# Selective-scan block: where the factor B of a state step is applied (rows of delta u on ScalarE and GpSimd, or a diagonal inside TensorE's product)

## The chip, the cores and the metric

One NeuronCore of a Trainium2 chip runs the whole program. The metric is the device time of one execution in microseconds (us). The kernel before took 759.8 us, the median of 3 runs (757.31 to 759.98).

## What is computed

The input is x with 4 sequences of 1024 tokens and 128 channels. First comes a layer norm with scale and shift, then a Mamba-like block (`_selective_scan`) with 256 channels and 16 states, a gate and an output product, and after it a second layer norm and a mixture of 8 experts of which each token takes 2. The part that matters here, cut from the reference:

```python
xp = u @ x_proj_w
delta = softplus(xp[..., :64] @ dt_proj_w + dt_proj_b)
Bm = xp[..., 64:80]
Cm = xp[..., 80:]
dA = exp(delta[..., None] * A)
dBu = delta[..., None] * Bm[:, :, None, :] * u[..., None]
h = dA_t * h + dBu_t          # per token, for each channel d and state n
y = einsum('bdn,bn->bd', h, C_t)
```

For one state n, dBu is delta u, (token x channel), with each token's row multiplied by that token's B of state n. Everything is fp32.

## The kernel before

**Segments and steps.** The 4096 tokens are cut into 8 segments (SEGS) of 512 tokens; a sequence is 2 segments, so the odd segments (1, 3, 5, 7) go on from the state that the even one before them left. A segment has 16 steps, one for each state n, so there are 128 steps k. A step has 2 halves a of 128 channels each. A half of a step is called a gap; a segment has 32 gaps.

**A step, engine by engine.** delta u of a segment lies in `duT` with tokens on the partitions: 4 chunks (CS) of 128 tokens by 256 channels. B lies beside it in `BT`, one column per chunk and state.

- `scale_in(k)` multiplies the rows of duT by the step's column of BT and writes them to `S`. In segments 0 to 6 a ScalarE instruction scales one chunk of 256 channels (L976), and one GpSimd instruction scales the last chunks (L522): `pool_chunks(k)` gives GpSimd 1 and 2 chunks in turn in segments 0 and 1, and 1 in segments 2 to 6. ScalarE has the rest.
- `turn_in(k, a)` on TensorE turns the four scaled blocks of 128 tokens by 128 channels into channels by tokens with `turn`, a matmul in transpose mode (L571), into one of 3 PSUM banks (DBU_BANKS).
- `decay(k, a)` on ScalarE computes dA for one half (L987).
- `scan(k, a)` on VectorE runs the recurrence over the 512 tokens (L1335): dA from SBUF, dBu from the PSUM bank, the result into `ring`.
- GpSimd multiplies both halves by the step's row of C (L542), which a DMA has spread over the partitions.
- `add_state(k, a)` on TensorE adds them up in PSUM with four more `turn` matmuls (L571), three steps later (LAG).

**The last segment is another case already.** In segment 7 `pool_chunks` is 0. ScalarE multiplies the identity matrix by the step's column of BT (L979), four 128x128 diagonals a step, and `turn_in` uses `product`, an ordinary fp32 matmul (L567), with the block of duT as the stationary operand and the diagonal as the moving one. That product scales and turns in one operation.

**Order.** Every engine runs a list written out by hand. Per gap TensorE issues `turn_in(k + 1, a)`, an `add_state`, and `gap_work`. ScalarE issues `scale_in(k + 2)` at the head of a step, then per half `decay(k + 2, a)` and `gap_work`. VectorE issues `scan(k, a)` and `gap_work`. GpSimd issues `scale_in(k + 2)`, the product with C, and its scatters. `gap_work` spreads the rest of the block over the gaps: `front` prepares the segment after (layer norm, two convolutions as 8 tap products of 512 columns, the gates), `project` computes its delta, B, C and duT (softplus needs an exponential and a logarithm, so ScalarE loads two function tables a segment, at gap 18), `tail` and `routing` work on the segment before (output product, second norm, router, choice of experts).

**What holds them together.** `turn_in(k, a)` waits for all of the step's scaling and for the scan that last used its bank, three halves back. `decay` waits for a scan six halves back (DA_SLOTS). `scale_in(k)` waits for step k - 3 to have been turned (S_SLOTS). At the first step of a segment `scale_in` waits on ScalarE and on GpSimd for `read["dT1"]`, which VectorE gives with the second half of duT (L1078, in gap 27). VectorE overwrites a duT slot only when the scaling of the segment two back is done. The expert part, from about 540 us on, uses the same engines one tile after another; it shares the memory of S.

Of the kernel before, what the change touches and what calls it, by code (L numbers as in the profile page):

```python
# [7 lines left out]
ALU = mybir.AluOpType  # L8
ACT = mybir.ActivationFunctionType
# [3 lines left out]
P = 128  # L13
BATCH, SEQ, HID = 4, 1024, 128
MLP, NSTATE, DTRANK, CONVK = 256, 16, 64, 4
EXPERTS, INTER, TOPK = 8, 352, 2
NTOK = BATCH * SEQ
HALVES = MLP // P
# [6 lines left out]
LN_EPS = 1e-5  # L25
PROJ = DTRANK + 2 * NSTATE
GAPS = 2 * NSTATE
RING, S_SLOTS, DBU_BANKS, DA_SLOTS, C_GROUP, LAG = 6, 3, 3, 6, 4, 3

INNER = [(c * P, min(P, INTER - c * P)) for c in range(-(-INTER // P))]  # L30
NIN = len(INNER)
# [16 lines left out]
def wait(eng, signal, count):  # L48
    if not (isinstance(count, int) and count <= 0):
        eng.wait_ge(signal, count)  # L50


def pool_chunks(k):

    s = k // NSTATE
    return 1 + k % 2 if s < 2 else int(s < SEGS - 1)


def act_scaled(k):

    return sum(CS - pool_chunks(j) for j in range(k + 1))


def pool_scaled(k):
    return sum(pool_chunks(j) > 0 for j in range(k + 1))


def adaln_kernel(nc, xT_d, w1_d, w2_d, wo_d, xproj_d, dtw_d, alog_d, conv_d, cols_d, bo_d, router_d,
# [5 lines left out]
    with ctx:  # L74
        def sb(name, shape, dt=fp32):
            return ctx.enter_context(nc.sbuf_tensor(name, shape, dt))

        def sem(name):
            return ctx.enter_context(nc.semaphore(name))
# [63 lines left out]
        soft = sb("soft", [P, 3, HALVES, BANK])  # L143
        rv, ev, lw = (soft[:, k] for k in range(3))
        delta = sb("delta", [P, 2, HALVES, BANK])
        S = sb("S", [P, S_SLOTS, CS, MLP])
        dA = sb("dA", [P, DA_SLOTS, BANK])
        Cb = sb("Cb", [P, 2, C_GROUP, BANK])
        ring = sb("ring", [P, RING, HALVES, BANK])
# [56 lines left out]
        def db(k, a):  # L206
            return bank(2 + (k * HALVES + a) % DBU_BANKS)
# [17 lines left out]
        def PO(k):  # L225
# [20 lines left out]
        av_ready, e_ready, lw_ready, w_ready, softplus_step, delta_ready = (  # L246
            sem(n) for n in ("av_ready", "e_ready", "lw_ready", "w_ready", "softplus_step", "delta_ready"))
        c_stored, c_loaded = sem("c_stored"), [sem(f"c_loaded{k}") for k in range(2)]
        scaled_act, scaled_pool, turned_in, da_ready, scanned, kept, prod_ready, summed, y_out, x1_ready = (
            sem(n) for n in ("scaled_act", "scaled_pool", "turned_in", "da_ready", "scanned", "kept", "prod_ready", "summed",  # L250
                             "y_out", "x1_ready"))
        route, prob_exp, chosen_ready, places_ready, place = (
            sem(n) for n in ("route", "prob_exp", "chosen_ready", "places_ready", "place"))
# [173 lines left out]
        def _(pool):  # L427
# [83 lines left out]
                        scatter_ready(f)  # L511
                    scatter(f, (gap - 9) // 3 // TOPK, (gap - 9) // 3 % TOPK)

            def scale_in(k):
                s, n = divmod(k, NSTATE)
                own = pool_chunks(k)
                if own:
                    if n == 0:
                        pool.wait_ge(read["bt"], s + 1)
                        pool.wait_ge(read["dT1"], s + 1)  # L520
                    wait(pool, turned_in, HALVES * (k - S_SLOTS + 1))
                    nc.gpsimd.tensor_tensor(S[:, k % S_SLOTS, CS - own:, :], duT[:, s % 2, CS - own:, :],  # L522
                                            BT[:, s % 2, CS - own:, n:n + 1].to_broadcast([P, own, MLP]), ALU.mult
                                            ).then_inc(scaled_pool, 1)

            pool.wait_ge(mod_step, MOD_STEPS)
            for window in (-2, -1):
                for gap in range(GAPS):
                    gap_work(gap, window)
            scale_in(0)  # L530
            scale_in(1)
            for k in range(STEPS):
                s, n = divmod(k, NSTATE)
                if k + 2 < STEPS:
                    scale_in(k + 2)
                pool.wait_ge(scanned, (k + 1) * HALVES)
                if s % SEG == 0:
                    nc.gpsimd.tensor_copy(state[:, n, :], ring[:, k % RING, :, BANK - 1]).then_inc(kept, 1)
                    pool.wait_ge(kept, s // SEG * NSTATE + n + 1)
                group_, own = divmod(k, C_GROUP)  # L540
                pool.wait_ge(c_loaded[group_ % 2], 16 * (group_ // 2 + 1))
                nc.gpsimd.tensor_tensor(ring[:, k % RING], ring[:, k % RING],  # L542
                                        Cb[:, group_ % 2, own, :].unsqueeze(1).to_broadcast([P, HALVES, BANK]),
                                        ALU.mult).then_inc(prod_ready, 1)
                gap_work(2 * n, s)
                gap_work(2 * n + 1, s)
# [18 lines left out]
        def _(pe):  # L565
# [3 lines left out]
            def turn(out, block_in, start=True, first=0):  # L569
                at = slice(first, first + block_in.shape[0])  # L570
                return nc.tensor.matmul(out, block_in, ident[at, at],  # L571
                                        is_transpose=True, start=start, stop=True, skip_group_check=True)
# [128 lines left out]
            def turn_in(k, a):  # L701


                if a == 0:
                    pe.wait_ge(scaled_act, act_scaled(k))
                    pe.wait_ge(scaled_pool, pool_scaled(k))
                wait(pe, scanned, HALVES * k + a - DBU_BANKS + 1)
                s = k // NSTATE
                for c in range(CS):
                    if s < SEGS - 1:  # L710
                        last = turn(db(k, a)[:, c * P:(c + 1) * P], S[:, k % S_SLOTS, c, a * P:(a + 1) * P])
                    else:
                        last = product(db(k, a)[:, c * P:(c + 1) * P], duT[:, s % 2, c, a * P:(a + 1) * P],
                                       S[:, k % S_SLOTS, c, 0:P])
                last.then_inc(turned_in, 1)

            def add_state(k, a):
# [141 lines left out]
        def _(act):  # L859
# [39 lines left out]
            def project(gap, f):  # L899
                if gap == 12:  # L900
                    act.wait_ge(filled["bt"], f + 1)
                    wait(act, scaled_pool, pool_scaled((f - 1) * NSTATE - 1))
                    nc.scalar.copy(BT[:, f % 2].rearrange("p c n -> p (c n)"), FB[:, 0:CS * NSTATE]).then_inc(read["bt"], 1)
                if gap in (5, 8):
                    a = (gap - 5) // 3
                    act.wait_ge(filled[f"dt{a}"], f + 1)
                    wait(act, delta_ready, f * HALVES)
                    nc.scalar.activation(ev[:, a, :], FB, ACT.Abs, bias=cols[:, 3, a:a + 1]).then_inc(av_ready, 1)  # L908
                    nc.scalar.activation(rv[:, a, :], FB, ACT.Relu, bias=cols[:, 3, a:a + 1]).then_inc(read[f"dt{a}"], 1)  # L909
                if gap in (9, 10):  # L910
                    a = gap - 9
                    act.wait_ge(av_ready, f * HALVES + a + 1)
                    nc.scalar.activation(ev[:, a, :], ev[:, a, :], ACT.Exp, scale=-1.0).then_inc(e_ready, 1)
                if gap == 18:
                    act.wait_ge(e_ready, (f + 1) * HALVES)
                    nc.scalar.activation(lw[:, :, :], ev[:, :, :], ACT.Ln, bias=1.0).then_inc(lw_ready, 1)  # L916
                if gap in (12, 21):
                    a = int(gap == 21)
                    act.wait_ge(read["bt"], f + 1)
                    wait(act, delta_ready, f * HALVES + a)  # L920
                    nc.scalar.activation(FB, ev[:, a, :], ACT.Identity, bias=1.0).then_inc(w_ready, 1)
# [46 lines left out]
            def scale_in(k):  # L968
                s, n = divmod(k, NSTATE)
                if n == 0:  # L970
                    act.wait_ge(read["bt"], s + 1)
                    act.wait_ge(read["dT1"], s + 1)
                wait(act, turned_in, HALVES * (k - S_SLOTS + 1))
                for c in range(CS - pool_chunks(k)):
                    if s < SEGS - 1:
                        nc.scalar.activation(S[:, k % S_SLOTS, c, :], duT[:, s % 2, c, :], ACT.Identity,  # L976
                                             scale=BT[:, s % 2, c, n:n + 1]).then_inc(scaled_act, 1)
                    else:
                        nc.scalar.activation(S[:, k % S_SLOTS, c, 0:P], ident[:, :], ACT.Identity,  # L979
                                             scale=BT[:, s % 2, c, n:n + 1]).then_inc(scaled_act, 1)  # L980

            def decay(k, a):
                s, n = divmod(k, NSTATE)
# [68 lines left out]
        def _(dve):  # L1052
# [15 lines left out]
            def project(gap, f):  # L1068
                if gap in (19, 20, 22, 23):
                    softplus((gap - 19) // 3, (gap - 19) % 3, f)  # L1070
                if gap in (25, 27):
                    a = (gap - 25) // 2
                    dve.wait_ge(filled[f"dT{a}"], f + 1)
                    dve.wait_ge(read[f"uT{a}"], f + 1)
                    if f > 1:
                        dve.wait_ge(scaled_act, act_scaled((f - 1) * NSTATE - 1))
                        dve.wait_ge(scaled_pool, pool_scaled((f - 1) * NSTATE - 1))
                    V.tensor_tensor(duT[:, f % 2, :, a * P:(a + 1) * P], uT[:, :, a * P:(a + 1) * P],  # L1078
                                    FB.rearrange("p (c d) -> p c d", c=CS), ALU.mult).then_inc(read[f"dT{a}"], 1)

# [431 lines left out]
```

## Time and profile before

| | |
|---|---|
| median of 3 runs | 759.8 us |
| profiled execution, its own time | 758.83 us |
| its span, first to last instruction | 756.2 us |
| granted TensorE clock, mean | 0.966 |
| busy share: TensorE, its weight loads, VectorE, ScalarE, GpSimd | 85%, 71%, 73%, 71%, 72% |
| first scan, last step of the chain that feeds the experts | 64.0 us, about 540 us |

The busy shares are averages over the set-up, the 128 steps and the experts. The five numbers lie close together, so they don't say which engine sets the pace of a stage; that is read from the start times of instructions that follow each other and from the waits. A TensorE matmul's duration in the trace holds its latency, so a row of "x4" lasts longer than it keeps the next one waiting: the distance between two starts is what one costs.

### The profile page before, as it was taken

The page shows a single profiled execution, that of the slowest core. Times are in us where ns is not written, and L with a number is a line of the kernel's source. Part 1 is how long each engine was busy: PE and PEld are TensorE (multiplying, and loading weights), DVE is VectorE, ACT ScalarE, POOL GpSimd, SP SyncE. Part 2 cuts the span into 40 slices and gives each one's busy share as a digit, 9 for nine tenths or more (in the row PEclk, how much of TensorE's full clock was granted, in tenths as well). Part 3 has the DMA queues.
Part 4 walks back from the last instruction along what each step waited for, and adds up shares of the span by engine and source line. Part 5 has one row for each costly group of instructions (what it writes and reads, how often), then busy time and mean ns, then how long its engine had stood idle before and what let it go on. Part 6 is the DMA issues. An engine that isn't in the chain of part 4 may idle for free.

```text
span 756.2 us, 14740 instructions
## 1 busy us (share of the span) xinstructions
PE 639.5 (85%) x4563; PEld 537.0 (71%) x4563; DVE 551.7 (73%) x1170; ACT 538.6 (71%) x1024; POOL 542.3 (72%) x519
## 2 busy tenths in 40 slices
PE   3768899989888989988988985899688997899994
PEld 3334766867857767766776774889577886899983
DVE  5066779899888998987989988999544574365552
ACT  3167989979987997996997997868226644465640
POOL 3055979989899899999999999978615454544431
PEclk9999999999999999999999999999789999999997
DMA  6020345355534633643344433586011122222544
GB/s 218 2 112 2 95 111 151 100 155 185 165 97 122 166 96 97 170 118 101 91 122 125 128 94 96 150 224 160 23 34 55 56 61 59 65 67 63 151 151 146
DMA packets 72492, 82.93 MB, mean 110 GB/s; under 512 B 7088, under 2 KB 63472, under 8 KB 68320
## 3 DMA queue, kind: packets, MB, share of 16 engines
q1 hardware_dynamic: 66944, 70.78, 34.6%
q0 software_dynamic: 4320, 9.12, 3.5%
q10 hardware_dynamic: 1152, 2.10, 0.7%
q8 instruction: 38, 0.62, 0.3%
q14 instruction: 38, 0.31, 0.1%
HBM read 52.19 MB, written 29.78 MB: 108 GB/s over the span
## 4 chain that ended last, share of the span: by engine, by line
PE 41%; ACT 32%; DVE 10%; issue 9%; POOL 3%; another core or an unknown queue 2%; DMA 2%; SPq 0%; ACTq 0%; DVEq 0%; POOLq 0%
PE psum L567 24%; PE psum L571 16%; ACT S L976 11%; ACT dA L987 10%; DVE ring L1335 4%; POOL ring L542 1%; ACT xn L881 1%; ACT L916 1%; ACT soft L908 1%; ACT soft L916 1%; ACT soft L909 1%; ACT L987 1%; ACT u L886 1%; ACT hT L863 1%
## 5 line engine op out<-in xcount | busy, mean ns | idle before, releaser
L542 POOL TENSOR_TENSOR ring<-ring,Cb 128x1024 f32<-128x1024 f32 x128 | 302.9, 2368 | 15.7 <-DVE ring L1335 10.4
L987 ACT ACTIVATE dA<-delta,A 128x512 f32<-128x512 f32 x256 | 178.6, 716 | 12.1 <-DVE ring L1335 12.0
L571 PEld LDWEIGHTS psum<-ident,S 128*128 128x128 f32 x896 | 107.4, 145 | 109.9 <-issue 75.8
L571 PE MATMUL psum<-ident,S 128*128 128x128 f32 x896 | 142.1, 284 | 45.8 <-issue 24.6
L571 PE MATMUL psum<-ident,ring 128*128 128x128 f32 x1088 | 164.5, 283 | 12.4 <-DMA ring<-results 6.7
L1335 DVE TENSOR_TENSOR_SCAN ring<-dA,state,psum 128x512 f32<-128x512 f32 x128 | 158.0, 1266 | 1.4 <-PE psum L571 1.0
L1335 DVE TENSOR_TENSOR_SCAN ring<-dA,psum 128x512 f32<-128x512 f32 x128 | 150.6, 1207 | 10.8 <-PE psum L571 6.8
L976 ACT ACTIVATE S<-duT,BT 128x256 f32<-128x256 f32 x320 | 139.3, 502 | 26.5 <-DVE duT L1078 17.8
L559 POOL DMA_INDIRECT results<-xn,result_at x71 | 68.7, 968 | 108.7 <-DVE xn L1462 68.1
L571 PEld LDWEIGHTS psum<-ident,ring 128*128 128x128 f32 x1088 | 132.7, 147 | 14.2 <-DMA ring<-results 7.4
L567 PE MATMUL psum<-uT,S 128*128 128x128 f32 x852 | 109.7, 280 | 0.5 <-issue 0.5
L567 PEld LDWEIGHTS psum<-uT,S 128*128 128x128 f32 x852 | 103.0, 196 | 1.5 <-issue 1.5
L1031 ACT COPY S<-gateup_w 128x736 f32 x71 | 57.0, 804 | 45.5 <-PE psum L567 37.8
L522 POOL TENSOR_TENSOR S<-duT,BT 128x256 f32<-128x256 f32 x112 | 75.7, 677 | 8.7 <-DVE duT L1078 7.7
L1467 DVE TENSOR_TENSOR S<-S,psum 128x384 f32<-128x384 f32 x71 | 39.3, 553 | 56.6 <-ACT S L1041 35.1
L454 POOL DMA_INDIRECT token_rows<-h2r,pos x64 | 65.0, 1016 | 17.6 <-issue 9.0
L1041 ACT ACTIVATE S<-psum 128x384 f32<-128x384 f32 x71 | 34.8, 490 | 56.2 <-PE psum L567 42.0
L567 PE MATMUL psum<-hT,w1c 128*128 128x512 f32 x128 | 67.7, 626 | 6.3 <-ACT u L886 3.5
L567 PE MATMUL psum<-soft,S 128*128 (+1 forms) x426 | 60.0, 277 | 9.9 <-DVE S L1467 6.3
L567 PEld LDWEIGHTS psum<-soft,S 128*128 128x128 f32 (+1 forms) x426 | 53.2, 192 | 11.4 <-issue 11.3
L1444 DVE COPY uT<-psum 128x128 f32<-128x128 f32 x71 | 20.5, 288 | 29.0 <-PE psum L571 18.7
L490 POOL TENSOR_SCALAR xT<-xT,gabo 128x1024 f32<-128x1024 f32 x4 | 11.4, 2871 | 35.5 <-PE psum L571 26.9
(229 smaller groups left out, 835.6 us busy)
## 6 DMA issues: line engine op xcount, KB each, us to landing
Cb<-c_rows SPq DMA_DIRECT2D x32, 1024.0 KB, 6.0
token_rows<-zeros SPq DMA_DIRECT2D x64, 272.0 KB, 7.0
uT<-token_rows SPq DMA_DIRECT2D x71, 68.0 KB
ring<-results SPq DMA_DIRECT2D x16, 256.0 KB, 3.4
xT<-in_xT SPq DMA_DIRECT2D x4, 512.0 KB, 5.2
out_T<-xT ACTq DMA_DIRECT2D x8, 256.0 KB
stage<-in_xT SPq DMA_DIRECT2D x6, 256.0 KB, 8.3
gateup_w<-in_gate SPq DMA_DIRECT2D x1, 1408.0 KB, 9.3
```

Of the source, the lines that this page charges most:

```text
L454: nc.gpsimd.indirect_dma_start(token_rows, bass.IndirectOffsetOnAxis(ap=pos[:, j, g * CS + c:g * CS + c + 1], axis=0), h2r[:, j, g * CS + ...
L522: nc.gpsimd.tensor_tensor(S[:, k % S_SLOTS, CS - own:, :], duT[:, s % 2, CS - own:, :], BT[:, s % 2, CS - own:, n:n + 1].to_broadcast([P, ...
L542: nc.gpsimd.tensor_tensor(ring[:, k % RING], ring[:, k % RING], Cb[:, group_ % 2, own, :].unsqueeze(1).to_broadcast([P, HALVES, BANK]), AL ...
L559: nc.gpsimd.indirect_dma_start(results, bass.IndirectOffsetOnAxis(ap=result_at[:, t % (2 * XS_SLOTS):t % (2 * XS_SLOTS) + 1], axis=0), ob[ ...
L567: return nc.tensor.matmul(out, lhsT, rhs, start=start, stop=stop)
L571: return nc.tensor.matmul(out, block_in, ident[at, at], is_transpose=True, start=start, stop=True, skip_group_check=True)
L976: nc.scalar.activation(S[:, k % S_SLOTS, c, :], duT[:, s % 2, c, :], ACT.Identity, scale=BT[:, s % 2, c, n:n + 1]).then_inc(scaled_act, 1)
L987: nc.scalar.activation(dA[:, (k * HALVES + a) % DA_SLOTS, :], delta[:, s % 2, a, :], ACT.Exp, scale=A[:, a, n:n + 1]).then_inc(da_ready, 1)
L1031: nc.scalar.copy(both_w[:, par % 2, :], gateup_w[:, ds(e * 2 * INTER, INTER + NIN * P)]).then_inc(weights_copied, 1)
L1041: nc.scalar.activation(silu[:, par % 2, :], PG(par)[:, 0:NIN * P], ACT.Silu).then_inc(silu_ready, 1)
L1335: V.tensor_tensor_scan(ring[:, k % RING, a, :], dA[:, (k * HALVES + a) % DA_SLOTS, :], db(k, a), state[:, n, a:a + 1] if s % SEG else 0.0, ...
L1467: V.tensor_tensor(innerT[:, par % 2, :], silu[:, par % 2, :], PU(par)[:, 0:NIN * P], ALU.mult).then_inc(inner_ready, 1)
```

## The change

In all segments ScalarE writes the four diagonals of a step, 128x128 each, and TensorE's `product` of duT with them scales and turns. S has 6 slots of half the width in place of 3, so its size is unchanged. GpSimd's `scale_in` is gone with its counts. TensorE waits for `read["dT0"]` and `read["dT1"]` itself at the first step of a segment, ScalarE no longer does; VectorE's wait before it overwrites duT is for TensorE's products.

```diff
-RING, S_SLOTS, DBU_BANKS, DA_SLOTS, C_GROUP, LAG = 6, 3, 3, 6, 4, 3
+RING, S_SLOTS, DBU_BANKS, DA_SLOTS, C_GROUP, LAG = 6, 6, 3, 6, 4, 3
...
-        S = sb("S", [P, S_SLOTS, CS, MLP])
+        S = sb("S", [P, S_SLOTS, CS, P])
...
-            def scale_in(k):
...
-                    nc.gpsimd.tensor_tensor(S[:, k % S_SLOTS, CS - own:, :], duT[:, s % 2, CS - own:, :],
-                                            BT[:, s % 2, CS - own:, n:n + 1].to_broadcast([P, own, MLP]), ALU.mult
-                                            ).then_inc(scaled_pool, 1)
...
             def turn_in(k, a):
+                s, n = divmod(k, NSTATE)
+                if n == 0:
+                    pe.wait_ge(read[f"dT{a}"], s + 1)
                 if a == 0:
-                    pe.wait_ge(scaled_act, act_scaled(k))
-                    pe.wait_ge(scaled_pool, pool_scaled(k))
+                    pe.wait_ge(scaled_act, CS * (k + 1))
                 wait(pe, scanned, HALVES * k + a - DBU_BANKS + 1)
-                s = k // NSTATE
                 for c in range(CS):
-                    if s < SEGS - 1:
-                        last = turn(db(k, a)[:, c * P:(c + 1) * P], S[:, k % S_SLOTS, c, a * P:(a + 1) * P])
-                    else:
-                        last = product(db(k, a)[:, c * P:(c + 1) * P], duT[:, s % 2, c, a * P:(a + 1) * P],
-                                       S[:, k % S_SLOTS, c, 0:P])
+                    last = product(db(k, a)[:, c * P:(c + 1) * P], duT[:, s % 2, c, a * P:(a + 1) * P],
+                                   S[:, k % S_SLOTS, c, :])
...
                 if n == 0:
                     act.wait_ge(read["bt"], s + 1)
-                    act.wait_ge(read["dT1"], s + 1)
                 wait(act, turned_in, HALVES * (k - S_SLOTS + 1))
-                for c in range(CS - pool_chunks(k)):
-                    if s < SEGS - 1:
-                        nc.scalar.activation(S[:, k % S_SLOTS, c, :], duT[:, s % 2, c, :], ACT.Identity,
-                                             scale=BT[:, s % 2, c, n:n + 1]).then_inc(scaled_act, 1)
-                    else:
-                        nc.scalar.activation(S[:, k % S_SLOTS, c, 0:P], ident[:, :], ACT.Identity,
-                                             scale=BT[:, s % 2, c, n:n + 1]).then_inc(scaled_act, 1)
+                for c in range(CS):
+                    nc.scalar.activation(S[:, k % S_SLOTS, c, :], ident[:, :], ACT.Identity,
+                                         scale=BT[:, s % 2, c, n:n + 1]).then_inc(scaled_act, 1)
...
                     if f > 1:
-                        dve.wait_ge(scaled_act, act_scaled((f - 1) * NSTATE - 1))
-                        dve.wait_ge(scaled_pool, pool_scaled((f - 1) * NSTATE - 1))
+                        dve.wait_ge(turned_in, HALVES * (f - 1) * NSTATE)
```

## Rows read from the trace of the kernel before

**Rows 1.** The page's parts 1 and 4: busy time, and the chain by engine.
```profile
PE 639.5 (85%) x4563; PEld 537.0 (71%) x4563; DVE 551.7 (73%) x1170; ACT 538.6 (71%) x1024; POOL 542.3 (72%) x519
PE 41%; ACT 32%; DVE 10%; issue 9%; POOL 3%; another core or an unknown queue 2%; DMA 2%; SPq 0%; ACTq 0%; DVEq 0%; POOLq 0%
```

**Rows 2.** Windows: the stretch, its length, busy us (and instructions) by engine, granted clock.
```profile
61.00:119.00 58.00, 48.93 (x317) 37.50 (x317) 44.46 (x46) 54.30 (x105) 50.02 (x47) 0.97 0.30 85
119.00:180.00 61.00, 56.97 (x397) 44.57 (x395) 55.96 (x71) 55.90 (x111) 57.29 (x44) 1.00 0.42 119
302.00:363.00 61.00, 53.89 (x369) 42.88 (x367) 52.10 (x80) 54.00 (x108) 57.24 (x62) 0.97 0.45 120
424.00:479.00 55.00, 41.41 (x306) 35.07 (x305) 48.44 (x76) 46.48 (x91) 51.41 (x56) 0.97 0.48 125
479.00:540.00 61.00, 56.41 (x478) 53.16 (x475) 56.45 (x109) 44.54 (x101) 53.08 (x36) 1.00 0.55 142
```

**Rows 3.** The scans (L1335), all of them, then timeline rows at two segment starts.
```profile
L1335 DVE TENSOR_TENSOR_SCAN ring<-dA,psum x128: 1185/1209/1223, 64.0 to 480.5; 128x512 f32<-128x512 f32 x128
L1335 DVE TENSOR_TENSOR_SCAN ring<-dA,state,psum x128: 1248/1270/1281, 119.4 to 534.4; 128x512 f32<-128x512 f32 x128
...
421.53 2.32 DVE L1335 TENSOR_TENSOR_SCAN ring<-dA,psum 128x512 f32<-128x512 f32 x2
...
481.63 2.42 DVE L1335 TENSOR_TENSOR_SCAN ring<-dA,state,psum 128x512 f32<-128x512 f32 x2
```

**Rows 4.** Groups by line and shape: busy us, mean ns, idle before and its releasers.
```profile
L571 PE MATMUL psum<-ident,S 128*128 128x128 f32 x896 | 142.1, 284 | 45.8 <-issue 24.6 <-ACT S L976 14.6 <-POOL S L522 3.3
L976 ACT ACTIVATE S<-duT,BT 128x256 f32<-128x256 f32 x320 | 139.3, 502 | 26.5 <-DVE duT L1078 17.8 <-PE psum L571 6.0 <-issue 2.7
L567 PE MATMUL psum<-S,duT 128*128 128x128 f32 x256 | 34.6, 279 | 1.8 <-DVE ring L1335 1.6
L979 ACT ACTIVATE S<-ident,BT 128x128 f32<-128x128 f32 x64 | 20.2, 387 | 2.6 <-DVE duT L1078 2.6
L522 POOL TENSOR_TENSOR S<-duT,BT 128x256 f32<-128x256 f32 x96 | 59.1, 616 | 8.7 <-DVE duT L1078 7.7
L522 POOL TENSOR_TENSOR S<-duT,BT 128x512 f32<-128x512 f32 x16 | 16.7, 1044 | 0.0
```

**Rows 5.** TensorE's timeline in segment 4: start, us, line, operation and its operands.
```profile
342.50 1.00 PE L571 MATMUL psum<-ident,S 128*128 128x128 f32 x4 [2.15 <-ACT S L976]
343.30 1.06 PE L571 MATMUL psum<-ident,ring 128*128 128x128 f32 x4
344.16 1.06 PE L571 MATMUL psum<-ident,S 128*128 128x128 f32 x4
...
350.05 0.60 PE L571 MATMUL psum<-ident,ring 128*128 128x128 f32 x4
350.48 1.02 PE L567 MATMUL psum<-hT,w1c 128*128 128x512 f32 x2
351.35 0.60 PE L571 MATMUL psum<-ident,S 128*128 128x128 f32 x4
```

**Rows 6.** TensorE's timeline in segment 7.
```profile
482.73 1.06 PE L567 MATMUL psum<-S,duT 128*128 128x128 f32 x8
483.62 0.60 PE L571 MATMUL psum<-ident,ring 128*128 128x128 f32 x4
484.06 1.06 PE L567 MATMUL psum<-S,duT 128*128 128x128 f32 x8
```

**Rows 7.** ScalarE's timeline, from segment 4's table load to its tanh; last, segment 7.
```profile
328.94 1.29 ACT L976 ACTIVATE S<-duT,BT 128x256 f32<-128x256 f32 x3
330.14 0.71 ACT L987 ACTIVATE dA<-delta,A 128x512 f32<-128x512 f32 x1
330.86 1.28 ACT L916 ACT_TABLE_LOAD   x1
...
340.20 0.66 ACT L886 ACTIVATE u<-psum,zhalf 128x512 f32<-128x512 f32 x1
...
496.28 1.26 ACT L979 ACTIVATE S<-ident,BT 128x128 f32<-128x128 f32 x4
497.45 0.71 ACT L987 ACTIVATE dA<-delta,A 128x512 f32<-128x512 f32 x1
```

More of the change, by code:

```diff
@@ L50, in wait @@
         eng.wait_ge(signal, count)
-def pool_chunks(k):
-    s = k // NSTATE
[L56 to L65, printed above, removed]
 def adaln_kernel(nc, xT_d, w1_d, w2_d, wo_d, xproj_d, dtw_d, alog_d, conv_d, cols_d, bo_d, router_d,
@@ L248, in adaln_kernel @@
         c_stored, c_loaded = sem("c_stored"), [sem(f"c_loaded{k}") for k in range(2)]
-        scaled_act, scaled_pool, turned_in, da_ready, scanned, kept, prod_ready, summed, y_out, x1_ready = (
-            sem(n) for n in ("scaled_act", "scaled_pool", "turned_in", "da_ready", "scanned", "kept", "prod_ready", "summed",
+        scaled_act, turned_in, da_ready, scanned, kept, prod_ready, summed, y_out, x1_ready = (
+            sem(n) for n in ("scaled_act", "turned_in", "da_ready", "scanned", "kept", "prod_ready", "summed",
                              "y_out", "x1_ready"))
@@ L512, in gap_work @@
                     scatter(f, (gap - 9) // 3 // TOPK, (gap - 9) // 3 % TOPK)
-            def scale_in(k):
[L515 to L521, printed above, removed]
-                    nc.gpsimd.tensor_tensor(S[:, k % S_SLOTS, CS - own:, :], duT[:, s % 2, CS - own:, :],
-                                            BT[:, s % 2, CS - own:, n:n + 1].to_broadcast([P, own, MLP]), ALU.mult
-                                            ).then_inc(scaled_pool, 1)
             pool.wait_ge(mod_step, MOD_STEPS)
@@ L529, in _ @@
                     gap_work(gap, window)
-            scale_in(0)
-            scale_in(1)
             for k in range(STEPS):
                 s, n = divmod(k, NSTATE)
-                if k + 2 < STEPS:
-                    scale_in(k + 2)
                 pool.wait_ge(scanned, (k + 1) * HALVES)
@@ L701, in turn_in @@
             def turn_in(k, a):
+                s, n = divmod(k, NSTATE)
+                if n == 0:
+                    pe.wait_ge(read[f"dT{a}"], s + 1)
                 if a == 0:
-                    pe.wait_ge(scaled_act, act_scaled(k))
-                    pe.wait_ge(scaled_pool, pool_scaled(k))
+                    pe.wait_ge(scaled_act, CS * (k + 1))
                 wait(pe, scanned, HALVES * k + a - DBU_BANKS + 1)
-                s = k // NSTATE
                 for c in range(CS):
-                    if s < SEGS - 1:
-                        last = turn(db(k, a)[:, c * P:(c + 1) * P], S[:, k % S_SLOTS, c, a * P:(a + 1) * P])
-                    else:
-                        last = product(db(k, a)[:, c * P:(c + 1) * P], duT[:, s % 2, c, a * P:(a + 1) * P],
-                                       S[:, k % S_SLOTS, c, 0:P])
+                    last = product(db(k, a)[:, c * P:(c + 1) * P], duT[:, s % 2, c, a * P:(a + 1) * P],
+                                   S[:, k % S_SLOTS, c, :])
                 last.then_inc(turned_in, 1)
@@ L901, in project @@
                     act.wait_ge(filled["bt"], f + 1)
-                    wait(act, scaled_pool, pool_scaled((f - 1) * NSTATE - 1))
                     nc.scalar.copy(BT[:, f % 2].rearrange("p c n -> p (c n)"), FB[:, 0:CS * NSTATE]).then_inc(read["bt"], 1)
```

## The prediction

> **What bounds the kernel now.** I read the page's shares and the chain first, then windows of one segment each, then the timelines of TensorE and ScalarE inside a segment. The busy shares of the five lie within 14 points and say little; the chain already says more: TensorE 41%, ScalarE 32%, GpSimd only 3% [rows 1]. So GpSimd's work, which the change takes away, is mostly off the path.
>
> The 128 steps run from the first scan at 64.0 us to the last at 534.4 + 1.27 = 535.7. Segment 0 takes 119.4 - 64.0 = 55.4 us, segments 1 to 5 take 421.5 - 119.4 = 302.1 (60.4 each), segment 6 takes 60.1 and segment 7 54.1 [rows 3]. In segments 1 to 5 ScalarE is busy 54 to 56 of 61 us, GpSimd 57, VectorE 52 to 56 [rows 2]. TensorE's busy figure of 54 to 57 overstates its load, since durations hold latency. Its true load comes from distances between starts: four turns take 350.48 - 350.05 = 0.43 us, 0.11 each, and a pair of 512-column products 351.35 - 350.48 = 0.87, 0.43 each [rows 5]. From the code a middle segment has 372 matmul instructions: 256 turns of turn_in and add_state, 84 other short ones, and 32 wide ones (an ordinary fp32 product is two instructions). The windows confirm the number: 397 and 369 in 61 us [rows 2]. So TensorE's floor is 340 x 0.11 + 32 x 0.43 = 37.4 + 13.8 = 51.2 us of 60.4. The 9 us left are waits, for ScalarE's scaling above all: turn_in's turns stood idle 45.8 us, 14.6 put down to L976, 3.3 to GpSimd's scaling and 24.6 to nothing seen [rows 4]; and stretches at half clock behind such waits, as at 343.30, where four turns take 0.86 us after a wait of 2.15 [rows 5]. ScalarE in turn waited 17.8 us at 5 places for VectorE's duT [rows 4]. The pace now is thus set by ScalarE, with TensorE 15% below its limit.
>
> **The change, part by part.**
>
> 1. *GpSimd's scaling goes*: 96 x 0.616 + 16 x 1.044 = 75.8 us of its time [rows 4]. TensorE waited for it 3.3 us in all. I take nothing for it beyond that, since the next point fills the gap: the cover is TensorE itself, which will be later than GpSimd was.
>
> 2. *ScalarE's scaling changes shape.* Three rows of 256 columns take 330.14 - 328.94 = 1.20 us, 0.40 each. Four diagonals take 497.45 - 496.28 = 1.17 us [rows 7]. In segments 2 to 6 that is the same work (-0.03 x 80 = -2 us). In segments 0 and 1 ScalarE had 2.5 chunks a step, 1.0 us: +0.17 x 32 = +5.4 us, on an engine with, after the change, over 5 us a segment to spare, so nothing on the path.
>
> 3. *ScalarE's wait for duT goes*, 17.8 + 2.6 us [rows 4]. It moves to TensorE, which asks for duT at gap 30, when the scan of gap 29, issued behind duT's gap 27 on VectorE, must be done for the bank anyway. Only a wait already there remains. At the very first segment it saves the three scalings between duT and the first turn, 1.2 us: **-1.2 us**. TensorE queues add_state and gap_work behind this wait; with nothing added to it, they lose nothing.
>
> 4. *TensorE: 8 turns a step become 8 ordinary fp32 products.* This is the main term. Segment 7 shows it: L567 with S and duT has 256 instructions, 16 steps x 8 products x 2 [rows 4], while in segments 0 to 6 the 7 x 16 x 8 = 896 turns are one instruction each. And each one costs the same as a turn: a half-step of 8 + 4 instructions comes every 484.06 - 482.73 = 1.33 us, 0.111 each [rows 6]. So a half gets 4 more instructions, a segment 128 more, 128 x 0.11 = 14.1 us.
>  - Segments 1 to 5: floor 51.2 + 14.1 = 65.3 us, which is above the 60.4 of now and above ScalarE (54), VectorE (52 to 56) and GpSimd (57 less 10). TensorE becomes the bound, and the waits for ScalarE are mostly absorbed, because the slower TensorE lets ScalarE run up to its limit of dA slots ahead.
>  - What can't be absorbed: the block around the two table loads. From 330.86 to 340.86 ScalarE needs 10.0 us for gaps 18 to 22 [rows 7]; TensorE will want 5 x 1.33 + 3 taps x 0.87 = 9.3 us for them and then waits for the tanh of gap 22. VectorE has its softplus in the same gaps. I allow 1.5 us there and 1 us elsewhere, 2.5 a segment. Bounds: 0 (segment 7's first six halves show none) and the 9 us of now.
>  - The half clock stretches cost now (1 - 0.97) x 61 = 1.8 us in a typical segment [rows 2]; they follow waits, and where waits are short (window 119 to 180 and segment 7) the clock is 1.00, so I expect them gone; they are part of the 9.
>  - Sum: 5 x (65.3 + 2.5) = 339.0 against 302.1: **+36.9 us**.
>  - Segment 0 has 317 instructions, 28 of them wide: 289 x 0.11 + 28 x 0.43 = 43.8; + 14.1 + 2.5 = 60.4 against 55.4: **+5.0 us**.
>  - Segment 6 prepares no further segment. Its count is 326, 14 wide: 312 x 0.11 + 14 x 0.43 = 40.3, + 14.1 = 54.4. That is below its 60.1 of now. VectorE, 48.4 of 55 us busy, or 53 of 60, is as close [rows 2]. I take 58.5: **-1.6 us** (bounds 55 and 60).
>  - Segment 7 and the experts stay: **0**.
>
> A rule from elsewhere stands against this. The Trainium skill, "TensorE: Matmul & The Clock Gate", Terms (entry xbus), says that transpose mode is 4x faster for FP32. By it each product would cost four turns and the sum would be 3 x 0.11 x 8 x 112 = 296 us. The trace disagrees: two turns, in a segment of the same kernel [rows 4, 6].
>
> 5. *Six slots of S, VectorE's wait for turned_in*: 0. ScalarE's scale_in is held by its place in the list behind decay, not by S (6.0 us of waits for it in all, [rows 4]); VectorE's new wait asks for products of the segment before the running one, done some 25 gaps earlier. No DMA is moved or added; SP's queue sees the same list, later.
>
> Sum: 36.9 + 5.0 - 1.6 - 1.2 = +39.1 us on the profiled execution's 758.8, so 797.9; that execution lies 1.0 under the median of 759.8, so I say **799 us**. (A change of 0.5%, 4 us, is about what can be told from none.)
>
> **The rivals.**
>
> *B: the waits stay on top.* TensorE's products come in bursts that wait for scans three halves back, and VectorE's own bursts then add to the longer work. For it: the idle time is now spread over ScalarE, VectorE and GpSimd, and most of turn_in's is put down to nothing [rows 4]. Against it: at the head of segment 7 TensorE runs without a hole. Price: 7 segments x 14.1 = +99, 858 us; half of it, 822 to 830, if only half is absorbed. Chance 0.08 beyond 822.
>
> *C: faster.* The place is the head of each segment and the table block, where TensorE now waits for ScalarE and ScalarE for duT. If ScalarE's waits of 17.8 + 2.6 us were the pace and TensorE had room for the products, the scan phase would fall by that: 739 us. The point from which it decides: TensorE's floor with the products under ScalarE's 54 us a segment, that is at most 25 added (2.8 / 0.11) instructions where 128 are counted, or a pace of a product under 0.13 us for the pair. Against it: 1.33 us per half in segment 7. Chance 0.03.
>
> *D: no difference*, 756 to 763 us: TensorE's load fits just into its present idle time, as if the 9 us a segment were all usable and my count of the 84 other instructions too high by 45. The windows' counts speak against it. Chance 0.03.
>
> *E: a product costs four turns* when it isn't in segment 7's calm: 759 + 296 = 1055 us. Nothing shows that. Chance 0.01.
>
> **How the numbers follow.** Forecast A (TensorE-bound, waits of 0 to 6 us a segment): with no waits at all and segment 6 at 57 the sum is 24.4 + 2.5 - 3 - 1.2 = +22.7, 782.5; with 6 us a segment, 6 x 3.5 = 21 more than taken, 820. Chance 0.85, of which about 0.81 lies within 785 to 821. The range is **785 to 821**. Slower 0.94 (A, B, E), same 0.03 (D), faster 0.03 (C).
>
> **What the profile would show.** L976 and L522 with S are gone, L979's line has 512 instructions at 0.387 us, L567 with S and duT has 2048. TensorE is over 92% packed in segments 1 to 5, with halves of 1.33 us plus gap_work; the distance between scans two segments apart grows from 121 to some 136 us; clock 1.00 there; GpSimd about 45 of 68 us busy, and its wait for scans up. TensorE's share of the chain rises over 60%, ScalarE's falls under 15%. Segment 7 still takes 54 us. I am wrong if segments 1 to 5 take under 63 us (the count or pace is off) or over 72 (the waits weren't absorbed), or if waits for scans show ahead of turn_in in most halves.

## The result and the profile after

The changed kernel takes 794.7 us (median of 4 runs, 794.17 to 798.23) against 759.9 for the kernel before: a ratio of 1.0469, 95% interval 1.0431 to 1.0507. The profiled execution took 794.17 us with a span of 792.2.

Parts 1 and 4 of the page of the kernel after, against [rows 1]:

```profile
PE 728.3 (92%) x5459; PEld 639.8 (81%) x5459; DVE 555.7 (70%) x1170; ACT 544.3 (69%) x1152; POOL 473.8 (60%) x407
PE 71%; DVE 9%; ACT 7%; issue 5%; POOL 2%; DMA 2%; another core or an unknown queue 1%; SPq 0%; ACTq 0%; DVEq 0%; POOLq 0%
```

TensorE has 5459 - 4563 = 896 more instructions (7 segments x 128) and 71% of the chain, up from 41%. ScalarE's share fell from 32% to 7%.

The scans and the starts of segments 6 and 7, against [rows 3]:

```profile
L1295 DVE TENSOR_TENSOR_SCAN ring<-dA,psum x128: 1184/1210/1222, 65.2 to 516.6; 128x512 f32<-128x512 f32 x128
L1295 DVE TENSOR_TENSOR_SCAN ring<-dA,state,psum x128: 1245/1271/1281, 124.4 to 570.5; 128x512 f32<-128x512 f32 x128
...
456.39 1.21 DVE L1295 TENSOR_TENSOR_SCAN ring<-dA,psum 128x512 f32<-128x512 f32 x1
...
517.74 1.26 DVE L1295 TENSOR_TENSOR_SCAN ring<-dA,state,psum 128x512 f32<-128x512 f32 x1
```

Read as before, they give each stage:

| stage | before | after | difference | forecast |
|---|---|---|---|---|
| start to first scan | 64.0 | 65.2 | +1.2 | -1.2 |
| segment 0 | 55.4 | 59.2 | +3.8 | +5.0 |
| segments 1 to 5 | 302.1 | 332.0 | +29.9 | +36.9 |
| segment 6 | 60.1 | 61.3 | +1.2 | -1.6 |
| segment 7 | 54.1 | 54.1 | 0 | 0 |
| last scan to end | 220.5 | 220.4 | -0.1 | 0 |

Windows of the kernel after, one segment each, against [rows 2]:

```profile
65.00:124.00 59.00, 58.52 (x436) 50.25 (x435) 44.70 (x44) 56.79 (x133) 39.21 (x32) 1.00 0.32 83
323.00:390.00 67.00, 67.00 (x502) 57.71 (x502) 53.63 (x84) 54.42 (x125) 49.72 (x47) 1.00 0.38 110
456.00:518.00 62.00, 59.34 (x473) 53.34 (x472) 53.19 (x84) 51.59 (x118) 48.53 (x45) 1.00 0.40 114
518.00:572.00 54.00, 52.05 (x443) 49.28 (x442) 51.68 (x91) 38.84 (x90) 45.60 (x31) 1.00 0.61 156
```

In segment 4 (323 to 390) TensorE is busy the whole 67 us, with 502 instructions where 500 were counted, at the full clock. The groups of the scaling, the product with C and the decay, against [rows 4]:

```profile
L511 POOL TENSOR_TENSOR ring<-ring,Cb 128x1024 f32<-128x1024 f32 x128 | 302.5, 2364 | 70.2 <-DVE ring L1295 64.3
L536 PE MATMUL psum<-S,duT 128*128 128x128 f32 x2048 | 274.5, 278 | 4.4 <-DVE ring L1295 4.0
L948 ACT ACTIVATE dA<-delta,A 128x512 f32<-128x512 f32 x256 | 178.2, 714 | 20.3 <-DVE ring L1295 18.2
L940 ACT ACTIVATE S<-ident,BT 128x128 f32<-128x128 f32 x512 | 162.3, 392 | 0.0
```

The 2048 product instructions had only 4.4 us of idle time ahead of them, all diagonals none, and the other engines now wait: GpSimd stands idle for 70.2 us ahead of its product with C, 64.3 of them for scans. In segments 1 to 5 (124.4 to 456.4 us) the list of TensorE's waits for matmuls is empty, and the rows of its matmuls cover 332.00 of 332.00 us.

### The profile page after: what moved, and what is told of

Read it like the earlier page. It is cut to its first block, busy times and chain, and to the rows that moved or that the text cites. A ratio compares the mean times of both kernels' runs of the same rounds, so it can differ in the third digit from the quotient of the medians.

```text
span 792.2 us, 16528 instructions
## 1 busy us (share of the span) xinstructions
PE 728.3 (92%) x5459; PEld 639.8 (81%) x5459; DVE 555.7 (70%) x1170; ACT 544.3 (69%) x1152; POOL 473.8 (60%) x407
## 4 chain that ended last, share of the span: by engine, by line
PE 71%; DVE 9%; ACT 7%; issue 5%; POOL 2%; DMA 2%; another core or an unknown queue 1%; SPq 0%; ACTq 0%; DVEq 0%; POOLq 0%
PE psum L536 52%; PE psum L540 17%; DVE ring L1295 3%; ACT dA L948 2%; ACT S L940 2%; PE psum L700 1%; POOL ring L511 1%; DVE S L1427 1%; ACT xn L848 1%; DMA ring<-results 1%; POOL token_rows L439 1%; DMA bo<-in_bo 0%; DVE psum L1047 0%; ACT S L1002 0%
## 5 line engine op out<-in xcount | busy, mean ns | idle before, releaser
L511 POOL TENSOR_TENSOR ring<-ring,Cb 128x1024 f32<-128x1024 f32 x128 | 302.5, 2364 | 70.2 <-DVE ring L1295 64.3
L536 PEld LDWEIGHTS psum<-S,duT 128*128 128x128 f32 x2048 | 255.0, 192 | 58.8 <-issue 43.5
L536 PE MATMUL psum<-S,duT 128*128 128x128 f32 x2048 | 274.5, 278 | 4.4 <-DVE ring L1295 4.0
L540 PE MATMUL psum<-ident,ring 128*128 128x128 f32 x1088 | 158.8, 276 | 11.7 <-DMA ring<-results 6.1
L940 ACT ACTIVATE S<-ident,BT 128x128 f32<-128x128 f32 x512 | 162.3, 392 | 0.0
L540 PEld LDWEIGHTS psum<-ident,ring 128*128 128x128 f32 x1088 | 128.1, 143 | 13.6 <-DMA ring<-results 6.7
L536 PEld LDWEIGHTS psum<-uT,S 128*128 128x128 f32 x852 | 104.6, 198 | 1.2 <-issue 1.2
L536 PE MATMUL psum<-soft,S 128*128 (+1 forms) x426 | 62.0, 283 | 8.6 <-DVE S L1427 7.8
L536 PEld LDWEIGHTS psum<-soft,S 128*128 128x128 f32 (+1 forms) x426 | 54.9, 197 | 10.1 <-issue 9.9
L507 POOL COPY state<-ring 128x2 f32<-128x2 f32 x64 | 12.0, 187 | 67.5 <-DVE ring L1295 67.3
```

The source lines that it names most:

```text
L536: return nc.tensor.matmul(out, lhsT, rhs, start=start, stop=stop)
L540: return nc.tensor.matmul(out, block_in, ident[at, at], is_transpose=True, start=start, stop=True, skip_group_check=True)
L940: nc.scalar.activation(S[:, k % S_SLOTS, c, :], ident[:, :], ACT.Identity, scale=BT[:, s % 2, c, n:n + 1]).then_inc(scaled_act, 1)
```

## The experiments

"Before" in each comparison is the kernel before, run on the same chip beside it; its medians there lay between 757.5 and 759.1 on three chips, so a difference between two experiments of 1 to 2 us says little.

**1. One instruction in place of two.** The changed kernel; the factor B is left out of the result.

```diff
-                    last = product(db(k, a)[:, c * P:(c + 1) * P], duT[:, s % 2, c, a * P:(a + 1) * P],
-                                   S[:, k % S_SLOTS, c, :])
+                    last = turn(db(k, a)[:, c * P:(c + 1) * P], duT[:, s % 2, c, a * P:(a + 1) * P])
```

> The changed kernel, but turn_in turns the block of duT against the identity in transpose mode: one TensorE instruction where the product is two. ScalarE still writes all four diagonals and TensorE still waits for them, but nothing reads them, so the factor B is left out of the result. Theory (TensorE's added instructions are the loss): its floor falls back to 51 us a middle segment, ScalarE's 54 us set the pace without the wait for duT, segments 1 to 5 take 56 to 59 us and the whole 730 to 748 us, under both kernels. Rival (the loss is in the new division of work: four diagonals on ScalarE, TensorE waiting for duT itself): the time stays at 785 to 795.

Measured: 737.1 us, 0.9707 of before (0.9677 to 0.9738). Its scans and one segment's window:

```profile
L1294 DVE TENSOR_TENSOR_SCAN ring<-dA,psum x128: 1182/1208/1221, 65.1 to 457.6; 128x512 f32<-128x512 f32 x128
L1294 DVE TENSOR_TENSOR_SCAN ring<-dA,state,psum x128: 1245/1269/1281, 121.8 to 510.2; 128x512 f32<-128x512 f32 x128
...
292.00:349.00 57.00, 53.85 (x376) 42.47 (x375) 52.92 (x84) 54.09 (x125) 49.80 (x46) 1.00 0.47 129
```

Everything else of the change is in place, ScalarE's four diagonals and TensorE's own waits too, and 57.6 us are gone. So the added TensorE instructions are the whole loss and more. (The edit takes them out of segment 7 too, where the kernel before has them: that segment takes 52.7 us here and 54.1 before.) The run also says that before was held back by something which this kernel lacks: in segments 0 to 6 it has TensorE's work of before, and its segments 2 to 5 take 57 us, not 60 to 63. Segment 1 takes 56.1 in both.

**2. More of the same.** The changed kernel with four more transposes a half:

```diff
                 for c in range(CS):
+                    turn(db(k, a)[:, c * P:(c + 1) * P], duT[:, s % 2, c, a * P:(a + 1) * P])
+                for c in range(CS):
                     last = product(db(k, a)[:, c * P:(c + 1) * P], duT[:, s % 2, c, a * P:(a + 1) * P],
```

> The changed kernel with four more transposes a half, of the same duT blocks into the same bank ahead of the products: 128 more TensorE instructions in each of the 8 segments, nothing added elsewhere. Theory (TensorE's instruction count sets the pace of segments 0 to 5): 14 us more in each of segments 0 to 5, 11 to 14 in 6 and 7 in which VectorE covers some: +105 to +113, 900 to 908 us. Rival (the pace is set by the round of three banks, scan and product): VectorE's wait hides part of it, under +85.

Measured: 893.3 us, 1.1758 of before (1.1722 to 1.1794), 98.6 over the changed kernel. Its scans and one segment's window:

```profile
L1297 DVE TENSOR_TENSOR_SCAN ring<-dA,psum x128: 1184/1214/1222, 64.4 to 606.7; 128x512 f32<-128x512 f32 x128
L1297 DVE TENSOR_TENSOR_SCAN ring<-dA,state,psum x128: 1244/1273/1282, 136.2 to 670.8; 128x512 f32<-128x512 f32 x128
...
296.00:376.00 80.00, 80.00 (x628) 70.59 (x627) 56.26 (x84) 55.24 (x125) 47.41 (x31) 1.00 0.32 92
```

The scans now span 672.1 - 64.4 = 607.7 us against 506.6: 101 us for 1024 instructions, 0.099 each, or 90% of the pace of one. A middle segment takes 80 us where it took 66 to 67, the full price; segments 6 and 7, where VectorE is close, hide a third (10 us each). The total is 7 us under the lower end of what was expected. Some 2 us of that are segments 6 and 7 (19.7 us more, where 22 to 28 were said) and 1 to 2 segment 0 (12.6 more, where 14 were said); the rest is spread thin, and some of it lies outside of the steps.

**3. GpSimd's scaling kept**, into a spare tile that nobody reads, with its old waits, in the changed kernel:

```diff
+                    nc.gpsimd.tensor_tensor(spare[:, 0:own, :], duT[:, s % 2, CS - own:, :],
+                                            BT[:, s % 2, CS - own:, n:n + 1].to_broadcast([P, own, MLP]), ALU.mult
+                                            ).then_inc(spared, 1)
```

> The changed kernel, and GpSimd still scales the chunks of the kernel before, in its old places and with its old waits, into a spare tile that nobody reads (96 x 0.62 + 16 x 1.04 = 76 us of its time). Theory: GpSimd has 17 to 28 us free in each segment, so 794 to 797 us. Rival (GpSimd's relief gave back part of the loss): up to 76 us more where its product with C comes late, and over 800 in any case.

Measured: 793.4 us (792.2 to 796.6), 1.0471 of before (1.0435 to 1.0507). With TensorE the bound, 76 us of GpSimd work cost nothing. The waits that are back are GpSimd's for duT and those of ScalarE and VectorE for it; TensorE does not wait for what nobody reads.

**4. The old waits back**: S with three slots in use and ScalarE's wait for duT, in the changed kernel.

```diff
                     act.wait_ge(read["bt"], s + 1)
+                    act.wait_ge(read["dT1"], s + 1)
```

> The changed kernel with three slots of S in use in place of six and with ScalarE's wait for duT back at the head of a segment. Theory: both are waits of an engine that has 10 us a segment to spare, 794 to 797 us. Rival (removing ScalarE's 18 to 20 us of waits for duT is what kept the loss at 35 where 14.1 x 7 = 99 us of instructions were added): 805 to 815.

Measured: 796.9 us, 1.0499 of before (1.0471 to 1.0528). In its trace the scans span 506.6 us, as in the kernel after. The two intervals overlap, so the 2.2 us can't be told from none, and in the profiled executions what is longer lies behind the last scan (224.9 us against 220.4).

**5. Segment 6 alone** with diagonals (and 7), in the kernel before.

```diff
+def diagonal(k):
+    s, n = divmod(k, NSTATE)
+    return s >= SEGS - 2
...
-                    if s < SEGS - 1:
+                    if not diagonal(k):
```

In this and the next experiments TensorE waits for duT itself in diagonal steps, and GpSimd scales nothing in them.

> The kernel before with diagonals and products in segments 6 and 7, not in 7 alone. In the changed kernel segment 6 took 61.4 us where it took 60.1. Theory: TensorE's floor there is 56 us, and with VectorE's softplus it comes to 61: 759 to 763 us. My forecast for this part was -1.6 us: 757 to 759.

Measured: 760.5 us, 1.0023 of before (1.0006 to 1.0040): +1.7, with segment 6 at 61.3 us in its trace as in the kernel after. The forecast of a gain there was wrong.

**6. Segment 7 in rows**, as all the others, in the kernel before.

> The kernel before with segment 7 also scaled in rows: ScalarE three chunks, GpSimd one, TensorE turns. Segment 7 then shows what turns and products are worth in a segment that VectorE bounds. Theory: with products it is VectorE-bound at 54.1 us and ScalarE has no duT wait; with turns ScalarE's wait of some 3.6 us for duT comes back and the rest stays: +2 to +6, 761 to 765 us. Rival (fewer TensorE instructions always pay): under 757.

Measured: 760.2 us, 1.0017 of before (0.9993 to 1.0041); segment 7 takes 53.5 us in place of 54.1, where a rise was expected. The total makes no difference that can be told. The edit moves two things at once, 128 TensorE instructions out of the segment and GpSimd's scaling into it; with the instructions out and no scaling (experiment 1) it takes 52.7. So even there they are worth up to 1.4 us of their 14.1, and VectorE covers the rest.

**7 and 8. Diagonals in the first step, or the first two, of each segment.** The kernel before, the choice of form by step (`n < 2` for two):

```diff
+def diagonal(k):
+    s, n = divmod(k, NSTATE)
+    return s == SEGS - 1 or n < 1
```

> The kernel before, with diagonals and products in the first step of each segment only (and in segment 7), where ScalarE stood waiting for duT 3.6 us. TensorE gets 8 instructions more a segment, 0.9 us, in its 9 us of idle time. Theory: ScalarE, which sets the pace before, loses most of its waits for duT (segments 1 to 6): -10 to -20 us, 739 to 749. Rival (TensorE's instructions cost their time wherever they are): +5, 764.

> The same with the first two steps of each segment. Theory: the wait for duT is gone whole, as the third step's scaling comes 4 us later; TensorE has 1.8 us more a segment, still within its idle time: 735 to 747, at or below the run with one step. Rival: +10, 770.

Measured: 757.4 us with one step, 0.9982 of before (0.9958 to 1.0006), and 765.3 with two, 1.0073 (1.0051 to 1.0096). Neither expected gain came, and the rivals (764 and 770) were too high as well. With one step ScalarE's 17.8 us of waits for duT are gone from the list of waits, whole, and the time didn't move: they were idle time of an engine that did not set the pace. (The step also takes 0.6 to 1.0 us a segment from GpSimd and gives 0.9 to TensorE, so this run alone doesn't prove it; experiment 10 asks about the waits by themselves.) And with the second step each of segments 1 to 6 is 0.6 to 1.0 us longer in the trace than with one, about the price of its 8 instructions (0.9): the heads of segments have no room on TensorE. That is 5 of the 7.9 us between the two medians; the rest lies elsewhere.

**9 to 11. What set the pace of before.** Since the one-pass kernel ran at 57 us a segment, what before had and it had not was put back: GpSimd's scaling (experiment 3's edit), the old waits (experiment 4's), and both. B is left out as in experiment 1.

> The one-pass kernel of the first run (turns of duT itself, B left out, ScalarE's diagonals made and waited for but not read: 737 us) with GpSimd scaling its old chunks into a spare tile. It asks why a kernel with the TensorE work of before takes 57 us a middle segment where before took 60.4 to 62.7. If GpSimd's load set the pace of the even segments of before (57 of 61 us busy, its copies of the state only there), the even segments rise to 61 to 63 and the time to 750 to 757. If ScalarE's waits did, it stays at 735 to 741.

> The one-pass kernel (737 us, B left out) with three slots of S in use and ScalarE's wait for duT back. If these waits made the 20 us between it and the kernel before: 750 to 757. If GpSimd's load did: 735 to 741.

> The one-pass kernel (B left out) with both put back: GpSimd's scaling into a spare tile, three slots and ScalarE's wait for duT. TensorE alone does not wait for GpSimd's scaling. Either theory: 753 to 760, as the kernel before, whose parts are then all there.

Measured: 759.9 us with GpSimd's scaling (1.0002 of before, 0.9982 to 1.0023), 738.9 with the waits (0.9735, 0.9697 to 0.9773), 758.7 with both (0.9989, 0.9969 to 1.0008). So GpSimd's scaling alone is worth the 22 us between the one-pass kernel and before, though nothing reads what it writes here. The first of the three came out above its expectation (750 to 757), because the odd segments and the last ones rose too, not the even ones alone: segments 2 to 7 take 59.6, 58.0, 62.6, 60.5, 58.6 and 56.6 us, where the one-pass kernel has 56.9 four times, 53.4 and 52.7, and before 62.7, 60.4, 62.4, 60.5, 60.1 and 54.1. The sums agree better than the parts: before loses more in segments 2, 3 and 6, this run more in 7.

What GpSimd's scaling holds up in the kernel before, the trace shows directly. TensorE's wait of 2.15 us at 342.50 is put down to ScalarE's scaling [rows 5]. It is ahead of the turns of step 12 of segment 4. Counting the scalings of both engines step by step, these are that step's two parts (steps are counted from 0):

```profile
335.44 1.29 ACT L976 ACTIVATE S<-duT,BT 128x256 f32<-128x256 f32 x3
341.79 0.61 POOL L522 TENSOR_TENSOR S<-duT,BT 128x256 f32<-128x256 f32 x1
```

ScalarE's part was done at 336.73, 5.8 us before the turns, and GpSimd's at 342.40, 0.10 us before them. Paired like this over all 112 steps, 43.3 of the 45.8 us of idle time ahead of turn_in's turns [rows 4], in 36 places, end 0.10 us after GpSimd's scaling of the same step, and ScalarE's was done 0.7 us or more earlier each time (3.1 or more from segment 2 on). The page gives 3.3 us of that to GpSimd, 14.6 to ScalarE and 24.6 to nothing. With one diagonal step (experiment 7), which took ScalarE's waits away, 36.6 us of these waits for GpSimd were left.

Why GpSimd is late, its own timeline in segment 4 says, which the prediction did not look at:

```profile
303.65 2.37 POOL L542 TENSOR_TENSOR ring<-ring,Cb 128x1024 f32<-128x1024 f32 x1
305.99 0.60 POOL L522 TENSOR_TENSOR S<-duT,BT 128x256 f32<-128x256 f32 x1
306.54 0.18 POOL L538 COPY state<-ring 128x2 f32<-128x2 f32 x1
306.80 2.37 POOL L542 TENSOR_TENSOR ring<-ring,Cb 128x1024 f32<-128x1024 f32 x1
309.12 0.61 POOL L522 TENSOR_TENSOR S<-duT,BT 128x256 f32<-128x256 f32 x1
309.68 0.18 POOL L538 COPY state<-ring 128x2 f32<-128x2 f32 x1
309.94 2.36 POOL L542 TENSOR_TENSOR ring<-ring,Cb 128x1024 f32<-128x1024 f32 x1
```

No row has a wait. A step is 306.80 - 303.65 = 3.15 us of GpSimd, 50.4 a segment, and its 8 scatters of 1.02 us and small operations for the layer norm fill most of the rest of the 62.4. The copy of the state, 306.80 - 306.54 = 0.26 us a step, is made in even segments only; before had 62.7 and 62.4 us in segments 2 and 4 and 60.4 and 60.5 in 3 and 5. (16 copies are 4.2 us and the difference is 2, so in the odd segments GpSimd's list is not the only limit.) In the one-pass kernel with GpSimd's scaling, which nothing waits for on TensorE, the delay comes through GpSimd's other work. TensorE's add_state waits for the product with C:

```profile
L558 PE MATMUL psum<-ident,ring 128*128 128x128 f32 x1088 | 162.7, 280 | 25.4 <-POOL ring L529 17.1 <-DMA ring<-results 6.4 <-DVE xT L1452 1.1
```

In the steps alone that is 13.0 us, and 11.7 more are for the layer norm's `xn`, which waits for GpSimd's `trs`; without GpSimd's scaling (experiment 1) both are 0.5. A part of the 22 us is the clock: over the steps the granted clock was 0.99 in experiment 1 and 0.97 in experiment 9 (before 0.98, after 1.00), with half-clock stretches behind such waits. An estimate from these figures is 0.02 x 469 = 9 us at most.

**12. A mixture**, to use both: diagonals in 6 of 16 steps of segments 2 to 6.

```diff
+def diagonal(k):
+    s, n = divmod(k, NSTATE)
+    return s == SEGS - 1 or (s >= 2 and n in (5, 6, 7, 8, 14, 15))
```

> The kernel before, with diagonals and products in 6 of 16 steps (n = 5 to 8, 14 and 15) of segments 2 to 6, away from the heads of segments where TensorE is packed, and in segment 7. GpSimd, which has no gap in segment 4 of the kernel before, loses 6 x 0.62 = 3.7 us a segment; TensorE gets 6 x 0.88 = 5.3 us on a floor of 51.2. Theory (before was bound by GpSimd's own list, after by TensorE's, and a mixture lies between): segments 2 to 5 at 58 to 60 us in place of 60.4 to 62.7, 745 to 752 us, under both kernels. Rival (each product costs its time wherever it is put): 5 segments x 5.3 = +26, 785.

Measured: 763.4 us, 1.0077 of before (1.0054 to 1.0099). TensorE's waits in segments 2 to 6 of its trace:

```profile
PE psum L577 <- POOL S L528: 16.5, 9, 3.5
PE psum L573 <- DVE uT L1074: 2.5, 5, 0.7
```

TensorE still stands 16.5 us for GpSimd's scaling, at steps 12 and 13 (10 to 13 in segment 6), the last of the row steps between the diagonal ones. In the kernel before, the waits for it in these five segments are 39.9 us, counted as under 9 to 11. So 23 us of waits went, and 5 x 5.3 = 26 us of TensorE instructions came. Segments 2 and 4 take 63.1 us, 3 and 5 take 62.3. The expected 745 to 752 did not come, nor the rival's 785. No kernel tried that computes the whole beats the kernel before clearly.

## Why the prediction was right, and where not

**The result** lies inside the range, 4 us under the forecast of 799. The rivals B (858), D (no difference) and E (1055) did not come; C (faster) named 739 us, and experiment 1, in which the product is made one instruction, gives 737. That agreement is chance: C's price was ScalarE's waits of 20.4 us for duT, and with that wait back the kernel still takes 738.9 (experiment 10). The 22 us were GpSimd's. (Half of the added work of 99 us would have given 809, inside the range, and not the 822 to 830 that B says.)

**Part 4, the main term, right.** 128 more instructions a segment at 0.11 us: the windows have 502 for 500, and experiments 1 and 2 show the term from both sides, where taking 1024 away gives 57.6 us and adding as many again costs 98.6. The floor of 65.3 us for segments 1 to 5 became 66.4 (65.1 in segment 1, which has 488 instructions, and 66.2 to 67.2 in the others, with 498 to 502).

**The allowance of 2.5 us for waits was too large**: 332.0 / 5 - 65.3 = 1.1 us. The products' 4.4 us of idle time in the whole program are nearly all (4.0) for scans and in segments 1 to 5 no wait of a matmul is listed, so the table block, for which 1.5 us a segment were taken, costs nothing that shows. By parts the error of the sum is -7.0 us in segments 1 to 5 and -1.2 in segment 0, +2.8 in segment 6 and +2.4 at the start. That the total is only 4 us off is in part luck, as 8.2 us one way meet 5.2 the other way.

**Segment 6, wrong in sign.** The step that failed is the count: 326 instructions were taken, and the list gives 340 (256 turns, 16 of start_y, 36 other turns, 18 for router and prefix, 14 wide). With 128 added the floor is 454 x 0.11 + 14 x 0.43 = 56.0 us, not 54.4; of the 5.3 us from there to 61.3 the trace names 2.2 in four waits for scans and 0.5 for delta, at VectorE's softplus; it puts the rest down to nothing. 58.5 - 54.4 = 4.1 us had been allowed above the floor.

**The start, wrong by 2.4 us.** The forecast saved the three scalings between duT and the first turn. ScalarE's timeline of the kernel before shows what stood ahead of them:

```profile
61.28 0.69 ACT L886 ACTIVATE u<-psum,zhalf 128x512 f32<-128x512 f32 x1 [7.66 <-PE psum L567]
61.87 1.29 ACT L976 ACTIVATE S<-duT,BT 128x256 f32<-128x256 f32 x3
```

ScalarE waited 7.66 us for the second tap product and its tanh, which its list puts ahead of scale_in(0), and duT was there by then. So the removed wait was not the last to end, nothing was saved, and the first half's products take 0.44 us more than its turns. The kernels that start as before have the first scan at 63.5 to 64.2 us, those that start with diagonals and without ScalarE's wait at 64.4 to 65.2, and those with the wait back at 64.0 to 65.0. So the measured +1.2 is partly spread from one execution to the next.

**What bounds before: wrong.** The prediction said that ScalarE sets the pace, since the chain gives it 32% and GpSimd 3%, and that GpSimd's work is mostly off the path. Experiments 9 to 11 show the reverse: GpSimd's scaling is worth 22 us, ScalarE's waits for duT next to nothing (738.9 against 737.1 us, and experiment 7). The step that failed is the reading of the releasers: turn_in waits for two scalings, and where the page named ScalarE's or nothing, GpSimd's had ended last. TensorE waited for GpSimd 43.3 us, not 3.3. The chain goes back by the same releasers, which fits its 3% for GpSimd, but its single links were not checked. The size of the forecast survived because it rested on the floor of the engine that would be the bound after, which does not depend on what held before. "Part 1: nothing" was therefore true only under the cover that it named, TensorE later than GpSimd (experiment 3); the change is 57.6 us of TensorE time (experiment 1) less some 22 of relief for GpSimd (759.9 in experiment 9 against 737.1).

**The clock, right.** It is 1.00 in the four windows shown, where three of the five of before had 0.97 [rows 2]; the half-clock stretches behind waits [rows 5] are gone.

**Two turns, not four, right.** A product is two instructions of 0.11 us and a turn is one, here and in experiments 1 and 2. The Trainium skill, "TensorE: Matmul & The Clock Gate", Terms, says that transpose mode is 4x faster for FP32; no run here bears that out.

## What to carry to other kernels

Count instructions and take the distance between starts on the engine that gets the work: if that floor lies clearly above today's stage time and the other engines' loads, it gives the new time well, whatever the waits of today are (65.3 against 66.4 us here). Where another engine is close it doesn't: segment 6 took 61.3 on a floor of 56.0. To say what bounds a stage today, look at each engine's own timeline for a stretch without a gap. Where an instruction waits for two engines, compare when each of them was done, and don't trust the name in the list or the chain's shares; a long wait on a list of waits can be taken away whole without moving the time. Before an operation is moved to spare one engine, ask whether the new one issues it as one instruction or two.

## What was unexpected of the hardware

GpSimd's product and scaling of one chunk cost the same in every kernel, 2.362 to 2.371 us and 0.616 to 0.619 on average, whether VectorE and TensorE were packed or not, and scans kept 1.21 and 1.27 us with GpSimd's 76 us of scaling or without. A product's weight load lasts 192 ns against 145 for a transpose, and that did not show in the distance between starts, 0.11 us for both.
